# A graph layer on one core: the indexed stores of a unit also wait for the next unit's second filter layer

## The reference

```
h    = relu(layernorm(x)) @ W_in2f.T                       # 12500 x 128
Wij  = smu(edge_attr @ W_f1.T + b_f1) @ W_f2.T + b_f2      # 400000 x 128
Wij  = Wij * edge_weight[:, None]
x_ij = h[dst] * Wij
agg  = segment_sum(x_ij, src)                              # 12500 x 128
out  = x + smu(agg @ W_o1.T + b_o1) @ W_o2.T + b_o2
```

## Time and profile before

| | us |
|---|---|
| median of 3 timed runs (4103.52 to 4111.21) | 4107.2 |
| span of the profiled execution | 5749.3 |
| TensorE busy in it (mean granted clock 0.83) | 4327.1, 75% |
| VectorE | 3410.0, 59% |
| ScalarE | 2118.5, 37% |
| GpSimd | 3038.4, 53% |

### The profile page before, as it was taken

How to read it: one execution, slowest core, us unless ns; L and a number is a source line. 1 busy time by engine, 2 the same in 40 slices (tenths; PEclk the granted TensorE clock), 3 DMA queues, 4 the chain that set the end, 5 groups by cost and what they waited for, 6 DMA issues and landing times. The chain is left out here.

```text
span 5749.3 us, 112809 instructions
## 1 busy us (share of the span) xinstructions
PE 4327.1 (75%) x32406; PEld 3547.2 (62%) x32406; DVE 3410.0 (59%) x11848; ACT 2118.5 (37%) x7302; POOL 3038.4 (53%) x3173
## 2 busy tenths in 40 slices
PE   5666557777777777777777777777777887877778
PEld 4455446666666666666666666666666666666567
DVE  6555445555565555565555666665555666666667
ACT  3455333333333333333333333333333333333333
POOL 4555555555555555555555555555555555555553
PEclk7777777887787788887887888898888988888989
DMA  6354434444443443444443444444444445554446
GB/s 171 110 134 134 113 111 131 129 135 125 131 123 113 114 115 110 117 115 112 112 115 109 118 134 135 136 140 121 123 124 124 143 143 140 146 144 129 128 134 191
DMA packets 459438, 737.76 MB, mean 128 GB/s; under 512 B 87025, under 2 KB 255323, under 8 KB 458961
## 3 DMA queue, kind: packets, MB, share of 16 engines
q1 hardware_dynamic: 291462, 461.44, 30.7%
q0 software_dynamic: 100000, 206.60, 10.7%
q10 hardware_dynamic: 67626, 65.48, 3.5%
HBM read 465.36 MB, written 267.82 MB: 128 GB/s over the span
## 5 line engine op out<-in xcount | busy, mean ns | idle before, releaser
L581 POOL DMA_INDIRECT sorted_rows<-msg,row_idx x3125 | 2997.9, 959 | 2627.5 <-DVE msg L992 1739.1
L711 ACT ACTIVATE hg<-p_h,weight 128x128 f32<-128x128 f32 x3136 | 894.7, 370 | 3102.5 <-remote 2804.8
L1253 PEld LDWEIGHTS p_seg<-seg_hot,seg 128*128 128x128 f32 x8288 | 1206.5, 213 | 784.6 <-issue 781.9
L999 DVE CUSTOM_DVE_ANT_0 product<-onehot,p_pos,start_at 128x112 bf16<-128x112 bf16 x3136 | 846.0, 324 | 1392.8 <-remote 1356.7
L1253 PE MATMUL p_seg<-seg_hot,seg 128*128 128x112 f32 x8288 | 1275.6, 298 | 337.3 <-issue 318.7
L1208 PE MATMUL p_w<-w_f,act 128*128 128x128 f32 x6272 | 1144.1, 327 | 223.2 <-issue 215.2
L1208 PEld LDWEIGHTS p_w<-w_f,act 128*128 128x128 f32 x6272 | 983.2, 233 | 240.2 <-issue 237.9
L1202 PE MATMUL p_z<-attr,w_f 128*128 128x512 f32 x1568 | 985.9, 707 | 186.0 <-issue 110.9
L1219 PE MATMUL p_h<-win,pick 128*128 128x128 bf16 x9408 | 826.9, 250 | 293.3 <-ACT hg L711 210.9
L992 DVE TENSOR_TENSOR msg<-p_w,hg 128x512 f32<-128x512 f32 x784 | 539.0, 688 | 736.0 <-ACT hg L711 448.8
L1219 PEld LDWEIGHTS p_h<-win,pick 128*128 128x128 bf16 x9408 | 700.7, 114 | 326.1 <-issue 319.8
(11 more groups left out here) (110 smaller groups left out, 1715.7 us busy)
## 6 DMA issues: line engine op xcount, KB each, us to landing
seg<-sorted_rows SPq DMA_DIRECT2D x448, 322.5 KB
seg<-sorted_rows SPq DMA_DIRECT2D x196, 516.0 KB
ends<-ends SPq DMA_DIRECT2D x392, 256.0 KB
sorted_rows<-msg,row_idx POOLq DMA_INDIRECT x3125
sorted_rows<-zero_rows ACTq DMA_DIRECT2D x336, 129.0 KB
win<-h SPq DMA_DIRECT2D x392, 96.0 KB
attr<-in_attrT SPq DMA_DIRECT2D x392, 80.0 KB
seg<-sorted_rows SPq DMA_DIRECT2D x56, 387.0 KB
```

Source lines behind the costliest of these rows:

```text
L581: pool.indirect_dma_start(out=sorted_rows[:, :], out_offset=bass.IndirectOffsetOnAxis(ap=row_idx[:, slot, k:k + 1], axis=0), in_=msg[:, sl ...
L711: last = act.activation(hg[:, v, k, :], p_h[:, k, :], ACT.Copy, scale=weight[:, bass.ds(n.value(TILES_U, k), 1)])
L999: last = dve.tensor_tensor_reduce(out=product[:, k, :], in0=onehot[:, slot, k, :], in1=p_pos[:, 0:BUCKETS], scale=1.0, scalar=start_at[:, ...
L1253: last = pe.matmul(out, seg[:, it.slot, l * it.tiles + k, 0:F], seg_hot[:, it.slot, l * it.tiles + k, :], start=(k == 0), stop=(k == it.ti ...
```

## The change

One wait is added in `scatter`, ahead of a unit's four stores: they also wait until `s_w` has counted n+2, that is until the second filter layer of unit n+1 is done. It is left out for the last unit, which has no next one. `wait_for(pool, s_w, n, 1, 2)` waits for the value n + 2; in the hardware loops n is computed from the loop register.

```
@@ -576,6 +576,8 @@
                 wait_for(pool, s_idx, n, 1, 1)
                 wait_for(pool, s_key, n, 1, 1)
                 wait_for(pool, s_msg, n, 1, 1)
+                if n.i is not None or n.base + 1 < n_units:
+                    wait_for(pool, s_w, n, 1, 2)
                 pool.sem_inc(s_go, 1)
                 for k in range(tiles):
                     pool.indirect_dma_start(out=sorted_rows[:, :],
```

## The result

The changed kernel took 4114.9 us (median of 14 runs, 4110.65 to 4118.59) beside 4106.1 us of the kernel before (14 runs): ratio 1.0021, 95% interval 1.0013 to 1.0028, 8.9 us slower. The forecast was 4111.

A forecast was written before the change was run, and what follows sets the result against it. POOL's indexed stores, 5.05 us a unit, were taken as the bound. The wait itself 0, steady state 0 and start 4.1 us, added to 4107.2, gave 4111 us (chance 0.50); range 4100 to 4131 us.

The forecast's parts named there:

- The bound: POOL's indexed stores: 1.262 us from start to start, 5.05 us a unit, practically without a break outside the profiler.
- The long profile: Span 5749.3 us against median 4107.2: POOL's 482 waits for DVE's message were taken as gaps of the profiled run only.
- (a): POOL's sequencer, passing one more wait per unit: claimed 0 us, hidden behind queued stores; ends 0 and 478 us.
- (b): Steady state: the next unit's layer is done 3.2 to 10.0 us before POOL needs it, so 0 us.
- thin-lead rival: Lead used up at round changes, preparing steps or low PE clock; 16 places x 1.52 us, 4131 us; chance 0.11.
- (c): First units, before there is a lead: POOL's flow begins 4.1 us later; bounds nothing to 7.6 us.
- the first rival: Whole run: no effect, the last idle moment past the start or the layer in time there; 4107 us, chance 0.31.
- Shorter stores by the shared port: POOL's stores: the new phase removes all excess over 952 ns from DVE's work beside them; 4085 us, chance 0.05.
- What the profile after would show: Message waits turned into `p_w` waits of similar total, steps 1.26 us, fifth unit near 65 us, span within 20 of 5749.

The follow-up runs named there:

- k1_all_but_start: The added wait in every unit but the first 8 and the last; 4108.5 us beside 4106.0 for the kernel before, ratio 1.0008.
- g1_after_again: The changed kernel measured once more, nothing altered; 4112.3 us beside 4106.2 for the kernel before, ratio 1.0017.
- m1_start_only: The added wait only in the first 8 units; 4115.8 us beside 4108.4 for the kernel before, ratio 1.0017.
- g2_landed: Instead of the added wait, a unit's stores wait until the unit before's have landed; 6209.6 us beside 4106.2 for the kernel before, ratio 1.5124.

## Why the prediction was right, and where it was not

**The bound** (POOL's stores, 5.05 us a unit, without a pause): right for the first kind of chip, the one forecast. From the thirteenth unit of the changed kernel (103.17) to the last store the step is 1.268 us in the mean, 5 ns above the plain step: some 15 us of waits and of longer stores in 3,076 steps, no single step longer than 3.4 us. The Trainium skill (Perfetto Trace Analysis, "GPSIMD Engine Instruction") advises to time GpSimd by the spacing of starts and not by durations; by durations POOL is busy 74% of this span, by the spacing all of it between first and last store, and the second is what the result follows. The prediction's own sign for the bound, that a kernel with fewer stores runs faster, wasn't tried.

**The long profile** was read wrongly. "About one gap for every two units that the timed one cannot hold" took for an artefact what is the real behaviour of another kind of chip. It did little harm to the sum, because that was carried over by what the stores alone need, and the median was of a kind of chip where nothing else counts; that the result was measured on that kind too was luck, since on the second kind the same change gave 9%, far outside the range.

**(a) the wait itself, 0 us:** right. The step is 2071.95 - 2070.68 = 1.27 us across a unit's border and 2073.20 - 2071.95 = 1.25 us inside; k1_all_but_start bounds the cost of all waits after the start at 7 us (its interval's end, 0.0017 x 4106).

**(b) the steady state, 0 us:** right but for 1.6 to 2.05 us. The slack was put at 3.2 to 10.0 us; its median is 9.4, its least 0.93. The thin-lead rival, priced at 16 places x 1.52 us, is true at one place out of 16, for 1.6 to 2.05 us. Its deciding point (a disturbance longer than the lead) was the right one: a landing was waited for 9.8 us there. The bounds for a landing, 2.3 to 9.1 us, were taken from other transfers, and this one shows that the long end is real.

**(c) the start, 4.1 us within 0 to 7.6:** the right mechanism, its size too small by a quarter to a half. Without the wait the thirteenth unit's stores start at 96.64 us, with it in the first 8 units at 102.23, with it in all at 103.17 and, in g1_after_again, at 104.01: 5.6, 6.5 and 7.4 us. Only one trace of the first kind has the start without the wait. The measured losses are 8.9 and 6.0 us with the wait in all units and 7.3 with it at the start alone; each interval leaves out zero, so the first rival, nothing at all, is ruled out, though its 4107 was only 4 us from the forecast. The term took unit 4 with the wait (64.96) against unit 6 without (70.98) from a trace of the second kind. On the first kind unit 5 without the wait starts at 61.18 and flows from there, and unit 4 with it at 62.38, after which unit 5 is at 67.50: 6.3 us later. The start that I had read was that of the second kind, with its gaps in it; they made the kernel before look later, and so the loss smaller by 1.5 to 3.3 us (4.1 instead of 5.6 to 7.4). With the one place of (b) the change costs 6.5 + 2.05 = 8.5 us by the first profile after and 7.4 + 1.65 = 9.0 by g1_after_again, within the interval of both measurements of it.

**Shorter stores by the shared port:** no sign of it. Among traces of the first kind the stores took 959 ns in the median and 962 in the mean where the new phase is missing after the start (m1_start_only), and 958 to 959 and 960 to 963 where it is there:

```profile
L583 POOL DMA_INDIRECT sorted_rows<-msg,row_idx x3125: 954/959/1477, 34.2 to 4002.9; - x196
```

**What the profile after would show:** the fifth unit near 65 us (62.38) and steps of 1.26 us came; the span near 5749 and waits turned to `p_w` did not on this kind of chip. On the second kind they did: 120.0 us under the name of `p_w` and 759.5 us as "remote", of 1317, but with a total 457 us smaller, where I had "about the same total". That the wait could make the kernel faster there, by holding rows of stores apart, is a rival that I had not written down.

No version beats the kernel before on the first kind of chip. The wait in all units but the first 8 keeps what the change gives on the second (0.9095 and 0.9110) and costs no more than can be told on the first (1.0008).

## What to carry to other kernels

An engine that holds a kernel by the spacing of its instructions hides any wait that ends within its lead; such a wait costs at the start, where there is no lead, and wherever something uses the lead up. At the start it costs what it delays the moment from which the engine flows. Price that moment from the undisturbed units, and compare span and timed median first: when they differ by 40%, find out whether the profile is of the same kind of chip before calling its gaps an artefact. A change of the order between engines should be timed on more than one chip, since here one and the same wait costs 0.2% on one kind and gives 9% on another. And where a wait is put down to "remote", look for the signal among those that the engine waits for: it may be one of the kernel's own that came late.

## What was not expected of the hardware

The same program took 4106 us and 5762 to 5841 us, by chip, with TensorE's granted clock at 0.97 and 0.83 and the transfers' bytes the same (737.76 MB). In the slow case TensorE's signals reach ScalarE 7 us and more after its matmuls end in the profile, and single matmuls start 0.7 to 1.45 us apart instead of 0.1 us, while indexed stores run. And the stores of a unit are landed late: 3.5 us from the start of the last store to the next that waits for it, where the store itself keeps GpSimd for 1.26 us (g2_landed).
